# ScalarE seeds the exponent scores' PSUM banks with the transposed mask, in the second pass

## What is computed

```python
qh, kh, vh = (proj(q, Wq, bq), proj(k, Wk, bk), proj(v, Wv, bv))
scores = jnp.einsum('bhqd,bhkd->bhqk', qh, kh) / jnp.sqrt(jnp.float32(D_K))
scores = jnp.where(mask[:, None] == 0, jnp.float32(-1000000000.0), scores)
attn = jax.nn.softmax(scores, axis=-1)
ctx = jnp.einsum('bhqk,bhkd->bhqd', attn, vh)
concat = ctx.transpose(0, 2, 1, 3).reshape(bs, -1, INPUT_DIM)
return concat @ Wo.T + bo
...
x = x + jnp.tanh(g_xattn[1]) * _L1_xattn_ref(_layernorm(x, axis=-1), ctx_1024, ctx_1024, mask_BxSxS2_ik1, ...)
```

## Time and profile before

| | us |
|---|---|
| median of 3 runs | 2464.26 |
| lowest, highest | 2459.34, 2464.36 |
| the profiled execution | 2460.99 |
| its span in the trace | 2459.2 |
| from its first to its last mask matmul of pass B (L1035) | about 904 to 2317 |

### The profile page before, as it was taken

The page is one execution under the profiler, slowest core; times in us unless marked ns, Lnnn a source line. Parts: engine busy times, 40 slices in busy tenths (PEclk is TensorE's granted clock), DMA queues, the critical chain, the costliest instruction groups (busy, mean ns, idle before and its releaser), DMA issues. The chain is left out here.

```text
span 2459.2 us, 74014 instructions
## 1 busy us (share of the span) xinstructions
PE 2168.4 (88%) x25884; PEld 1537.5 (63%) x25884; DVE 1611.5 (66%) x3702; ACT 1430.5 (58%) x2375; POOL 1129.2 (46%) x1905
## 2 busy tenths in 40 slices
PE   3888888888888859999999999999999999999957
PEld 2666666666666547667666766666666666666635
DVE  4888888888888845555555555555554555555569
ACT  1788787887877734444444444544544444544469
POOL 2666666666666633433343343434333433434320
PEclk6999999999999979999999999999999999999989
DMA  2111111111111000000000000000000000000025
GB/s 70 45 40 43 40 41 43 40 41 42 39 43 43 15 21 21 21 18 21 18 21 18 19 20 18 21 18 21 17 21 18 21 18 18 21 18 21 4 85 189
DMA packets 95564, 80.56 MB, mean 33 GB/s; under 512 B 11392, under 2 KB 95360, under 8 KB 95360
## 3 DMA queue, kind: packets, MB, share of 16 engines
q1 hardware_dynamic: 95360, 77.44, 10.4%
HBM read 60.63 MB, written 16.78 MB: 31 GB/s over the span
## 5 line engine op out<-in xcount | busy, mean ns | idle before, releaser
L553 ACT ACTIVATE probs<-bank_exp 128x1024 f32<-128x1024 f32 x512 | 523.8, 1023 | 679.0 <-ACTq L552 679.0
L787 DVE TENSOR_REDUCE a_nmax<-bank_max 128x8 f32<-128x1024 f32 x512 | 625.7, 1222 | 330.9 <-DVEq L786 326.2
L1044 PE MATMUL bank_max<-UM,U 32*128 32x256 f32 x4096 | 588.7, 405 | 4.6 <-PEq L1079 2.5
L1051 PE MATMUL bank_exp<-UM,U 32*128 32x256 f32 x4096 | 531.1, 377 | 0.0
L510 POOL TENSOR_TENSOR ff_y<-ff_y,gamma_bc 128x256 f32<-128x256 f32 x128 | 92.8, 725 | 804.8 <-POOLq L509 804.8
L1068 PE MATMUL bank_o<-probs,V 128*17 128x128 f32 x8192 | 324.2, 275 | 127.4 <-PEq L1064 126.9
L1051 PEld LDWEIGHTS bank_exp<-UM,U 32*128 32x128 f32 x4096 | 391.9, 185 | 0.6
L1068 PEld LDWEIGHTS bank_o<-probs,V 128*17 128x17 f32 x8192 | 187.7, 96 | 275.7 <-issue 275.3
L1044 PEld LDWEIGHTS bank_max<-UM,U 32*128 32x128 f32 x4096 | 354.3, 186 | 8.6 <-issue 7.9
L1165 PE MATMUL bank_t<-spare,wT 128*128 128x128 f32 x2048 | 259.1, 280 | 0.9 <-PEq L1162 0.9
L1165 PEld LDWEIGHTS bank_t<-spare,wT 128*128 128x128 f32 x2048 | 241.3, 194 | 1.6 <-issue 1.6
(11 more groups left out here) (163 smaller groups left out, 4151.6 us busy)
## 6 DMA issues: line engine op xcount, KB each, us to landing
ctx<-in_ctx SPq DMA_DIRECT2D x256, 128.0 KB, 2.1
X<-in_x SPq DMA_DIRECT2D x128, 128.0 KB, 2.1
out_y<-X SPq DMA_DIRECT2D x64, 256.0 KB, 2.1
ff_qq<-in_mask_BxSxS_ik SPq DMA_DIRECT2D x128, 64.0 KB, 1.8
X<-in_L_xattn_Wq SPq DMA_DIRECT2D x1, 256.0 KB, 2.7
X<-in_L_xattn_Wk SPq DMA_DIRECT2D x1, 256.0 KB, 3.1
X<-in_L_xattn_Wv SPq DMA_DIRECT2D x1, 256.0 KB, 3.8
X<-in_L_xattn_Wo SPq DMA_DIRECT2D x1, 256.0 KB, 4.2
```

What stands on the lines that cost most here:

```text
L553: nc.scalar.activation(a_probs[n], exp_pair[:, :, :, :].rearrange("p i h t -> p (i h) t"), ACT.Exp, scale=SCALE).then_inc(probs_made, 1)
L787: return v.tensor_reduce(a_nmax[:, k2, n * H // 2:(n + 1) * H // 2], max_pair[:, :, :, :].rearrange("p i h t -> p (i h) t"), axis=AX.X, op ...
L1044: last = mm(max_pair[:, r % 2, 2 * c:2 * c + 2, :], U[now][32 * r:32 * r + 32, c, :], UM[now][32 * r:32 * r + 32, DC + c, :, :], start=not ...
L1051: last = mm(exp_pair[:, r % 2, 2 * c:2 * c + 2, :], U[before][32 * r:32 * r + 32, DC + c, :], UM[before][32 * r:32 * r + 32, c, :, :], sta ...
```

## The change

In pass B the four mask matmuls a step on the exponent scores are gone. In their place the mask is transposed by TensorE, with the shifts, into the same bank; ScalarE copies both out in one instruction of 640 columns instead of 512 (`sh_mask_T`); and after each exponential has read the two exponent banks, ScalarE writes the transposed mask over them, repeated for eight heads (`seed_exp`, 128x1024, bf16 to f32). The score matmuls accumulate onto it, and the shift matmuls come last and signal `scores`. TensorE waits for `exp_seeded` ahead of each `fill`. Since ScalarE's write must follow its own exponential, it waits for it (`act_own`) and sends `probs_made` itself. Two matmuls ahead of the pass write both exponent banks once (`primed`). On VectorE the first maximum, the normalised attention, the mask and U move ahead of the statistics' aggregation and of the maximum of n2.

```diff
+        sh_mask_T = [sb(f"sh_T{n}", [P, 5 * P], BF16)[:, :] for n in range(2)]
+        sh_T = [t[:, 0:4 * P] for t in sh_mask_T]
+        mask_T = [t[:, 4 * P:5 * P] for t in sh_mask_T]
...
+            def seed_exp(ring):
+
+                nc.scalar.activation(exp_pair[:, :, :, :].rearrange("p i h t -> p (i h) t"),
+                                     mask_T[ring].rearrange("p (o t) -> p o t", o=1).broadcast_to([P, H // 2, P]),
+                                     ACT.Copy).then_inc(exp_seeded, 1)
+
+            def exp_settled(n):
+                act.wait_ge(scores, 1)
+                act.sem_inc(scores, -1)
+                nc.scalar.activation(a_probs[n], exp_pair[:, :, :, :].rearrange("p i h t -> p (i h) t"), ACT.Exp,
+                                     scale=SCALE).then_inc(act_own, 1)
+
+            def probs_settled():
+
+                act.wait_ge(act_own, 1)
+                act.sem_inc(act_own, -1)
+                act.sem_inc(probs_made, 1)
+
             def step_b(i, k, live):
                 odd = k % 2 == 1
                 if live(-2):
-                    exp_pair_of(1)
+                    exp_settled(1)
                 if live(-1):
                     act.wait_ge(shift_Td, 1)
                     act.sem_inc(shift_Td, -1)
-                    nc.scalar.activation(sh_T[(k + 1) % 2], bank_tb[1][:, 0:4 * P], ACT.Copy).then_inc(shift_out, 1)
+                    nc.scalar.activation(sh_mask_T[(k + 1) % 2], bank_tb[1][:, 0:5 * P], ACT.Copy).then_inc(shift_out, 1)
+                if live(-2):
+                    probs_settled()
+                    seed_exp(k % 2)
                 if not odd and live(2):
                     act.wait_ge(n1_made, 1)
...
-                    exp_pair_of(0)
+                    exp_settled(0)
                 if live(-3):
                     act.wait_ge(cn_T, 1)
...
+                if live(-1):
+                    if live(-2):
+                        probs_settled()
+                    else:
+                        act.wait_ge(mask_T_made, 1)
+                        act.sem_inc(mask_T_made, -1)
+                    seed_exp((k + 1) % 2)
+                elif live(-2):
+                    probs_settled()
...
-                if before is not None:
+
+                def add_shift(start):
                     for r in (hi, hi + 1):
-                        mm(exp_pair[:, r % 2, :, :], ones_b[32 * r:32 * r + 32, :],
-                           sh_T[ring][32 * r:32 * r + 32, :], start=True, stop=False, skip_group_check=True)
+                        last = mm(exp_pair[:, r % 2, :, :], ones_b[32 * r:32 * r + 32, :],
+                                  sh_T[ring][32 * r:32 * r + 32, :], start=start, stop=False, skip_group_check=True)
+                    return last
+                if before is not None and not seeded:
+                    add_shift(True)
...
-                if before is not None and masked:
-                    for b in range(2):
-                        last = mm(exp_pair[:, b, :, :], mask_before, ident[:, :].rearrange("p (o t) -> p o t", o=1)
-                                  .broadcast_to([P, HG, P]), start=False, stop=True, skip_group_check=True)
-                    last.then_inc(scores, 1)
+                if before is not None and seeded:
+
+                    add_shift(False).then_inc(scores, 1)
...
-                fill(0, now, before, k % 2, *masks)
+                if live(-2):
+                    pe.wait_ge(exp_seeded, 1)
+                    pe.sem_inc(exp_seeded, -1)
+                fill(0, now, before, k % 2, True, mask_b[k % RING])
...
-                    last.then_inc(shift_Td, 1)
+                        nc.tensor.transpose(bank_tb[1][:, b * P:(b + 1) * P], sh[:, b * P:(b + 1) * P], ident[:, :])
+                    nc.tensor.transpose(bank_tb[1][:, 4 * P:5 * P], mask_b[(k + 3) % RING], ident[:, :])\
+                      .then_inc(shift_Td, 1)
```

More of the change, by code:

```diff
@@ L225, in build @@
         in_out = sem("in_out")
+        primed = sem("primed")
+        exp_seeded = sem("exp_seeded")
+        mask_T_made = sem("mask_T_made")
+        act_own = sem("act_own")
         bv_made = sem("bv_made")
@@ L894, in step_b @@
                     n_bn = mine(v.bn_stats(st6_b[n][:, 0:6], xs(i + 5)))
+                if live(0):
+                    max_pair_of(0, k % 2).then_inc(max_read, 1)
+                if live(-3):
+                    vec.wait_ge(attn_back, 1)
+                    vec.sem_inc(attn_back, -1)
+                    mine(v.reciprocal(rden[:, :], bank_oh[:, :, DH]))
+                    settle()
+                    attn_normed().then_inc(attn_read, 1)
+                if live(1):
+                    vec.wait_ge(mask_in[(k + 1) % 2], 16)
+                    vec.sem_inc(mask_in[(k + 1) % 2], -16)
+                    n_m = mine(v.tensor_scalar(mask_b[(k + 1) % RING], mask_i[(k + 1) % 2], 0.0, MASKED,
+                                               ALU.is_equal, ALU.mult))
+                    vec.wait_ge(qk_proj, 1)
+                    vec.sem_inc(qk_proj, -1)
+                    settle(n_m)
+                    if live(3):
+                        vec.sem_inc(mask_used, 1)
+                    v.tensor_tensor(U[(k + 1) % RING][:, :, :], bank_t[0][:, :].rearrange("p (c t) -> p c t", c=4),
+                                    bqk_T[:, :].rearrange("p (c o) -> p c o", o=1).broadcast_to([P, 4, P]),
+                                    ALU.add).then_inc(u_made, 1)
                 if odd and (live(5) or live(-5)) and (live(1) or live(-9)):
@@ L1027, in attn_transpose, with fill @@
                 last.then_inc(attn_back, 1)
-            def fill(n, now, before, ring, mask_now=None, mask_before=None):
-                masked = mask_now is not None or mask_before is not None
+            def fill(n, now, before, ring, seeded=False, mask=None):
                 lo, hi = 2 * n, 2 * (1 - n)
-                if now is not None and masked:
+                if now is not None and seeded:
                     for b in range(2):
-                        mm(max_pair[:, b, :, :], ident[:, :], mask_now.rearrange("p (o t) -> p o t", o=1)
+                        mm(max_pair[:, b, :, :], ident[:, :], mask.rearrange("p (o t) -> p o t", o=1)
                            .broadcast_to([P, HG, P]), start=True, stop=False, skip_group_check=True)
-                if before is not None:
+                def add_shift(start):
                     for r in (hi, hi + 1):
-                        mm(exp_pair[:, r % 2, :, :], ones_b[32 * r:32 * r + 32, :],
-                           sh_T[ring][32 * r:32 * r + 32, :], start=True, stop=False, skip_group_check=True)
+                        last = mm(exp_pair[:, r % 2, :, :], ones_b[32 * r:32 * r + 32, :],
[3 more added lines that the diff above has]
+                    add_shift(True)
                 for c in range(DC):
@@ L1045, in fill @@
                                       UM[now][32 * r:32 * r + 32, DC + c, :, :],
-                                      start=not masked, stop=True, skip_group_check=True)
+                                      start=not seeded, stop=True, skip_group_check=True)
                         if c == DC - 1:
@@ L1141, in _ @@
             pe.wait_ge(pass_ends[0], 5)
+            for b in bank_exp:
+                last = mm(b, ident[:, :], ident[:, :].rearrange("p (o t) -> p o t", o=1).broadcast_to([P, HG, P]),
+                          start=True, stop=True, skip_group_check=True)
+            last.then_inc(primed, 1)
             def step_b(i, k, live):
@@ L1145, in step_b @@
                 before = (k + 2) % RING if live(-2) else None
-                masks = (mask_b[k % RING] if live(0) else None, mask_b[(k + 2) % RING] if live(-2) else None)
                 if live(-1):
@@ L1179, in step_b @@
                 if live(-2):
-                    pe.wait_ge(probs_made, 1)
-                fill(1, now, before, k % 2, *masks)
+                    pe.wait_ge(exp_seeded, 1)
+                    pe.sem_inc(exp_seeded, -1)
+                fill(1, now, before, k % 2, True, mask_b[k % RING])
                 if live(-1):
@@ L1184, in step_b @@
                     pe.sem_inc(shift_out, -1)
+                    if not live(-2):
+                        pe.sem_inc(mask_T_made, 1)
                 if live(-3):
```

30 lines of the change are left out of this document (4 added, 26 removed).

## The result

The changed kernel takes 2509.34 us (median of 4 runs, 2505.73 to 2515.54) against 2461.8 (median of 4 runs of the kernel before, 2458.25 to 2464.36): the ratio is 1.0196, with a 95% interval of 1.0176 to 1.0216. It is slower by 2.0%, some 48 us. That is 22 us above the forecast of 2487 and inside the range of 2456 to 2525, but above the 2470 to 2500 that the forecast's own case covered.

What follows compares the result with a forecast made beforehand. The n2 chain over ScalarE, GpSimd and TensorE was taken to bound even steps and, after the change, odd ones too. 2461.0 + 26.4 - 6.7 + 1 + 3 = 2484.7; forecast 2487 us, range 2456 to 2525.

Steps and rivals of the forecast that it cites:

- the forecast's own case: Whole kernel: the write delays n2 and lengthens the chain that limits the steps; 2470 to 2500 us, chance 0.54.
- The bound: Second pass: the chain ScalarE, GpSimd, TensorE limits even steps (11.00 us); TensorE limits odd ones (10.66) by 0.60 us.
- n2 delayed by 1.04: ScalarE's queue, both kinds of step: write (0.93) and wider shift copy (0.11) make n2 and the head masks 1.04 us later.
- The price of the write: ScalarE's 128x1024 write into the exponent banks, two a step: 1.02 us long, costed at 0.93 us each.
- The no-change case: Rival: a cheap write, with the old time equalled at 0.73 us of engine time; 2455 to 2469 us, chance 0.10.
- The gain behind L1256: TensorE from L1206 (now L1256) to the next exponential: 0.45 + 0.07 = 0.52 us goes away.
- Steps without the chain: Five steps at the pass's start and three at its end gain 0.84 us each, -6.7 us.
- The clock: Loop ends of the second pass: two more dips of TensorE's granted clock, 1.7 us lost in each, +3 us.
- that rival: Each even step's 1.5 us wait is followed by a clock dip of 1.7 us: 102 more, 2587 us, chance 0.04.
- TensorE stayed the bound: Rival: later n2 does not move L1206; even steps 10.48, odd 9.82, 2372 us; chance 0.15, wholly or half.
- The dear write: Rival: a write costs 1.14 us, +52 instead of +26; 2510 to 2525 us, chance 0.17.

Runs made afterwards that it cites:

- The idle copy: The kernel before plus a ScalarE copy of 128x1024 to an unused SBUF tile behind the copy of the shifts, mask matmuls kept: 2550.45 us, ratio 1.0345.
- both edits: The changed kernel with n2 ahead of the write and xn on ScalarE, and the shift matmuls ahead of the scores on TensorE: 2378.31 us, ratio 0.965.

## Why the prediction was right, and where it was off

**The bound: right.** The limit in even steps was the chain from n2 over GpSimd to TensorE, where TensorE's weight loads stood idle for 0.35 us. The kernel before with n2 ahead of xn shows it by itself.

**n2 delayed by 1.04: right.** The exponential to the end of n2 takes 4.02 where 2.98 + 1.04 was worked out, and gamma starts 4.20 after it, not 3.15. The three other links of the chain, 0.18, 2.86 and 0.42, are those of before to 0.01. The idle copy shows that a delay of 0.95 by itself costs 85 us.

**The price of the write: right.** It takes 1032 ns, and what follows it starts 0.95 after its start (0.93 taken). The Trainium skill, ScalarE: Activation LUTs, under what each stage is for, has PSUM as the faster target: the traces agree, 1032 against 1057 ns for the copy to SBUF, though that one writes bf16 and the other f32. By the figures of the same page of the Trainium skill, under what ACT_TABLE_LOAD costs, for an ACTIVATE with immediate operands the write would hold the engine 0.95, an estimate that agrees with what was measured. The no-change case needed 0.73. ScalarE's busy time rose by 241 us and not by some 260: the product of count and length counts what overlaps with the next instruction.

**The gain behind L1256: too large.** It was to be 0.52; the part from L1256 to the next exponential went from 4.57 to 4.14, so 0.43. The removal was sized right, as the kernel before without its mask matmuls shows with 0.51; but I had costed the shift matmuls' move at nothing. From the first mask matmul to the transposes of the attention the first block took 2.16 before (1511.78 - 1509.62) and takes 1.82 now: 0.34 less instead of 0.45. In the order before, a bf16 shift matmul of 0.22 us opened the exponent stream; now both streams open with a float32 matmul, and the second one of each follows after 0.32. The experiment with the shifts first gets 0.09 a step back. This makes the even step 11.62 instead of 11.52 and the odd one 10.66 instead of 10.58: 60 x 0.18 = 11 us of what was missing.

**Steps without the chain: the gain too large, and at the end of the wrong sign.** They became 0.53 shorter, not 0.84. Apart from the block, the second half of the weighting starts later: its probabilities are signalled by hand after the exponential, and where TensorE is the limit no wait covers that, as it does at L1256. In the kernel before, the weighting starts 0.31 after the last transposes (959.31 to 959.62), in an early step of the changed one 0.44 after (960.32 to 960.76). At the end of the pass I had put three steps with a gain. There half of each step's work is gone, and nothing is left between the write and the block that waits for it. The changed kernel, TensorE, behind step 127:

```profile
2366.95 0.59 PE L1073 MATMUL bank_max<-ff_qT,ident 128*128 128x512 bf16 x2 [1.95 <-PEq L1228]
...
2380.66 2.08 PE L1268 MATMUL bank_m<-wT,ff_xy 128*128 128x256 f32 x4
```

The wait is 1.95 us, against 0.55 in the kernel before; later L1268 takes 2.08 where it took 1.13, so the clock has fallen. The stages from the last copy of the shifts to the end of the last output projection, of the changed kernel and then of the kernel before, show it in the column of the granted clock, 0.55 against 0.98:

```profile
2374.27:2400.50 26.23, 20.52 (x120) 11.80 (x120) 4.58 (x15) 11.10 (x17) 8.13 (x17) 0.55 0.00 1
```

```profile
2328.38:2345.75 17.37, 13.19 (x126) 7.68 (x126) 4.25 (x13) 7.87 (x14) 7.73 (x17) 0.98 0.01 1
```

From the copy of the shifts in step 128 to the end it is 139.2 us instead of 130.8. Every kernel that writes the banks has between 139.2 and 141.5 there, every one that does not 129.7 to 131.5, so the 8 to 10 us belong to the write and what came with it. The two stages above last 26.2 and 17.4 us, so the whole loss lies in them. 1.6 us of it are there when the first score block starts behind the copy (1.76 us against 0.16), which is the wait for the write. Nearly all of the rest arises while the changed kernel's TensorE is granted 1.2 GHz, from 2.7 us behind the copy on and for 47.8 us. The kernel before has such a fall too, but only 16.8 us behind the copy, when its work of the pass is almost done, and for 23.9 us. It is so in every kernel: with the write the clock falls 1 to 3 us behind the copy and is low for 44 to 48 us in all, without it 15 to 19 us behind, for 20 to 24 us. That the waits for the write bring the early fall about is not shown: no experiment changed the end of the pass alone.

**The clock: too small.** Instead of two more falls there are four in the pass, some of them of double length; the loop ends with the steps behind them, and stray falls in between, take 8 us more, not 3. The profiled execution, the slowest of the four, is 31 us above my sum of 2484.7. Of that the blocks are 11, the end of the pass 11 (8.4, and 2.5 counted there as gain), the early steps 2, the clock and the loop ends 5; 3 us lie before the pass, where nothing was changed. That the median missed by 22 and not by 31 is luck: I had put it 3.3 us above the profiled execution (2484.7 + 3.3 is 2488, where I wrote 2487), and it lies 6.2 below.

**The rivals.** The clock did not fall in every even step (10 falls in the pass, one of them inside a loop turn), so that rival is out, but the experiment with the shifts first has some of it. That TensorE stayed the bound is true of the kernel in which n2 goes first: there the steps are 10.13, and 9.93 with the shift matmuls first. The dear write was wrong in its price (1.14 us, where 0.95 was measured), though its time of 2510 was met by other terms. So the mechanism of the forecast was right, and its time was too low by terms that I had put at nothing or too small.

## What to carry to other kernels

Before a wait or a write is put into an engine's queue, list what stands behind it there and follow each of those to the engine that sets the time; an engine that is 58% busy can still hold the one instruction that everybody waits for. A stretch of idle time of a third of a microsecond in every second step was enough to show where that was, and comparing with steps that lack one instruction (here those before n2 exists) pointed at the culprit before any experiment. When an engine gets new work, put it behind whatever feeds the chain, not ahead of it. With the same instructions, n2 ahead of the two xn was worth 2.3% here, and n2 ahead of the write as well, 4.4%.

## What the runs showed of the hardware that was not expected

- Two score streams in different 32-row parts of TensorE's array: the second float32 matmul of a stream follows the first after 0.32 us, later ones after 0.21 to 0.22. A bf16 matmul in front takes 0.22 and leaves 0.21 to 0.22 for all that follow. The order was worth 0.09 us a step (11.63 to 11.54, 10.66 to 10.57, and 10.13 to 9.93 with both blocks counting).
- A kernel whose steps have shorter medians was not faster: the granted clock fell 18 times instead of 10 in the pass, which took back in some steps what all had gained. Its runs also spread over 12.5 us, those of the kernel before, timed beside it, over 5.4. In the kernel with both edits the fastest run, 2368.82 us, had a mean granted clock of 0.978 and the slowest, 2388.03 us, one of 0.964.
- A ScalarE write of bf16 to float32 in PSUM takes 1032 ns for 1024 columns, 25 ns less than a bf16 copy to SBUF of the same size (1057 ns).
- At the end of the pass the granted clock fell 1 to 3 us behind the last copy of the shifts in all six kernels that write the banks, and 15 to 19 us behind it in the four that do not.
